# Deep-and-cross ranker on one core: SyncE fetches 13 and ScalarE 8 embedding fields, the biases come by ScalarE, h2's copies are later

## What is computed

```python
x0 = emb[ids].reshape(ids.shape[0], -1)
x = x0
for i in range(cross_w.shape[0]):
    s = x @ cross_w[i]
    x = x0 * s[:, None] + cross_b[i] + x
h = jax.nn.relu(x0 @ w1 + b1)
h = jax.nn.relu(h @ w2 + b2)
h = jax.nn.relu(h @ w3 + b3)
logit = jnp.concatenate([x, h], axis=1) @ out_w + out_b
return jax.nn.sigmoid(logit)
```

## Time and profile before

| | us |
|---|---|
| median of 3 runs | 531.18 (529.99 to 531.2) |
| the profiled execution | 530.56 |
| its span, first to last instruction | 528.8 |
| PE busy | 480.8 (91%) |
| POOL busy | 379.6 (72%) |
| DVE busy | 186.4 (35%) |
| ACT busy | 84.7 (16%) |

### The profile page before, as it was taken

One profiled execution on the slowest core, in us unless ns is written; L12 is line 12 of the kernel. 1 busy time (PEld: TensorE's weight loads), 2 busy tenths in 40 slices (PEclk: granted clock), 3 DMA queues, 4 the chain that ended last, 5 costly groups with the idle time before them and its releaser, 6 DMA issues.

```text
span 528.8 us, 11324 instructions
## 1 busy us (share of the span) xinstructions
PE 480.8 (91%) x2912; PEld 442.2 (84%) x2912; DVE 186.4 (35%) x391; ACT 84.7 (16%) x159; POOL 379.6 (72%) x407
## 2 busy tenths in 40 slices
PE   2699899899999989899898989999899898999997
PEld 1399698898989889798887988888898888989996
DVE  5766414232142423224242321424232142423325
ACT  4642111111011111102011110101111010101111
POOL 5777776777777777777777777777777777777720
PEclk9999999999999999999999999999999999999999
DMA  7971111111111111111111111111111111111100
GB/s 234 387 263 29 28 29 27 28 29 27 29 29 29 28 28 30 29 29 29 27 29 26 30 27 30 26 30 29 26 30 25 30 27 28 27 28 28 28 10 2
DMA packets 19700, 24.90 MB, mean 47 GB/s; under 512 B 9305, under 2 KB 10292, under 8 KB 19636
## 3 DMA queue, kind: packets, MB, share of 16 engines
q0 software_dynamic: 12800, 13.13, 11.2%
q1 hardware_dynamic: 4770, 10.74, 5.7%
q10 hardware_dynamic: 2066, 0.31, 0.3%
HBM read 24.41 MB, written 0.01 MB: 46 GB/s over the span
## 4 chain that ended last, share of the span: by engine, by line
PE 55%; POOL 14%; issue 10%; ACTq 9%; DMA 5%; DVE 4%; ACT 3%; POOLq 0%; DVEq 0%
PE l_bank L717 41%; POOL x_raw L347 14%; ACTq L387 8%; DMA x_raw<-in_L_rec_emb,idx 4%; PE x_bank L717 4%; PE x_bank L729 4%; PE h_bank L771 3%; ACT xT_hi L400 2%; DVE x_raw L516 2%; ACTq L384 1%; PE l_bank L802 1%; DVE xT_lo L523 1%; PE h_bank L741 1%; DVE h2T_lo L528 1%; ACT h2T_hi L411 1%
## 5 line engine op out<-in xcount | busy, mean ns | idle before, releaser
L347 POOL DMA_INDIRECT x_raw<-in_L_rec_emb,idx x400 | 378.8, 947 | 125.5 <-issue 107.7
L717 PE MATMUL l_bank<-w_hi,xT_hi 128*128 128x342 f32 (+1 forms) x624 | 144.9, 333 | 3.5 <-DVE xT_lo L523 3.3
L717 PE MATMUL l_bank<-w_lo,xT_hi 128*128 128x342 f32 (+1 forms) x624 | 137.9, 321 | 0.0
L717 PE MATMUL l_bank<-w_hi,xT_lo 128*128 128x342 f32 (+1 forms) x624 | 137.7, 321 | 0.0
L717 PEld LDWEIGHTS l_bank<-w_hi,xT_hi 128*128 128x128 f32 x624 | 104.0, 191 | 7.9 <-DVE xT_lo L523 5.6
L717 PEld LDWEIGHTS l_bank<-w_lo,xT_hi 128*128 128x128 f32 x624 | 106.8, 191 | 0.0
L717 PEld LDWEIGHTS l_bank<-w_hi,xT_lo 128*128 128x128 f32 x624 | 106.3, 190 | 0.0
L523 DVE TENSOR_TENSOR xT_lo<-x_bank,xT_hi 128x512 fp32r<-128x512 f32 (+1 forms) x66 | 38.2, 578 | 158.5 <-ACT xT_hi L400 158.5
L400 ACT ACTIVATE xT_hi<-x_bank 128x512 fp32r<-128x512 f32 (+1 forms) x66 | 33.5, 507 | 270.3 <-PE x_bank L729 220.4
L729 PE MATMUL x_bank<-identity,x_raw 128*128 128x128 f32 x208 | 34.7, 279 | 27.0 <-DVE x_raw L516 27.0
L729 PEld LDWEIGHTS x_bank<-identity,x_raw 128*128 128x128 f32 x208 | 25.0, 142 | 36.7 <-issue 31.0
(11 more groups left out here) (94 smaller groups left out, 296.5 us busy)
## 6 DMA issues: line engine op xcount, KB each, us to landing
ids<-in_L_rec_emb SPq DMA_DIRECT2D x1152, 0.2 KB
ids<-in_L_rec_emb ACTq DMA_DIRECT2D x896, 0.2 KB
w_raw<-in_L_rec_w SPq DMA_DIRECT2D x18, 512.0 KB, 15.0
x_raw<-in_L_rec_emb,idx POOLq DMA_INDIRECT x400, 2.4
b_rows<-in_L_rec_b SPq DMA_DIRECT2D x1, 512.0 KB
b_rows<-in_L_rec_b SPq DMA_DIRECT2D x1, 256.0 KB
ids<-in_r_ids SPq DMA_DIRECT2D x1, 208.0 KB, 2.7
b_rows<-in_L_rec_b SPq DMA_DIRECT2D x1, 128.0 KB
```

Source lines behind the costliest of these rows:

```text
L347: pool.indirect_dma_start(out=dst, out_offset=None, in_=emb, in_offset=rows).then_inc(landed, 16)
L717: done = pe.matmul(bank[:, 0:b - a], x[:, k, :], w[:, k, a:b], start=(k == 0 and n == 0), stop=(k == last_k and n == 2))
```

## The change

- GpSimd leaves 21 fields to others instead of 16. SyncE takes field 21 of tiles 2 to 14 (13 fields), ScalarE field 20 of tiles 3, 5, 6, 8, 9, 11, 13 and 14 (8). Both lie in chunk 10, the last of group 2. Tile 15 is GpSimd's alone.
- ScalarE's shares become five, `[13, 19, 14, 16, 18]`, 80 rows a step; `fetch` may go over from one field to the next within a share, with a load for each, and stops after 8 x 128 rows.
- The placing copies come behind the copy of group 1 instead of group 2.
- On ScalarE, h2's copy moves from ahead of group 1's copy to behind it and the placing; on VectorE, h2's difference moves from ahead of group 1 to behind it. In the last step both stay.
- The five loads of biases go from SyncE's queue to ScalarE's, ahead of its copy of group 1 in the first step.
- The addresses are made by four instructions instead of three.

```diff
@@ -44,20 +44,21 @@
     LOW_BITS = 2 ** (H.bit_length() - 1) - 1
-    SP_TILES = [2, 4, 6, 8, 9, 10, 12, 14, 15]
+    SP_TILES = list(range(2, TILES - 1))
     SP_REGS = 32
-    SP_FIELD = F - 2
+    SP_FIELD = GROUPS[2][-1] * FPK + 1
     SP_BUFS = 4
-    assert SP_FIELD // FPK in GROUPS[-1] and SP_FIELD // FPK in LAST_GROUPS[3]
-    ACT_TILES = [3, 5, 7, 9, 11, 13, 15]
-    ACT_FIELD = F - 1
+    ACT_TILES = [3, 5, 6, 8, 9, 11, 13, 14]
+    ACT_FIELD = GROUPS[2][-1] * FPK
     ACT_BUFS = 2
-    ACT_SHARES = [8, 12, 4, 16, 12, 12]
-    assert ACT_FIELD // FPK in GROUPS[-1] and all(
-        sum(ACT_SHARES) * (t - 1) >= P * (j + 1) for j, t in enumerate(ACT_TILES)) and P % sum(ACT_SHARES) == 0
+    ACT_SHARES = [13, 19, 14, 16, 18]
+    assert all(sum(ACT_SHARES) * (t - 1) >= P * (j + 1) for j, t in enumerate(ACT_TILES))
+    ONE_RUNS = [(SP_FIELD, range(2, TILES - 1)), (ACT_FIELD, range(3, 10, 3)), (ACT_FIELD, range(5, 15, 3)), (ACT_FIELD, range(13, 14))]
+    AT_ROWS = [(f, t) for f, tiles in ONE_RUNS for t in tiles]
+    assert sorted(AT_ROWS) == sorted([(SP_FIELD, t) for t in SP_TILES] + [(ACT_FIELD, t) for t in ACT_TILES])
     ROW = E * 4
@@ -280,16 +280,14 @@
                 src = {"w1": w1, "w2": w2, "w3": w3}[name][k * P:(k + m) * P, :].rearrange("(m p) c -> p m c", m=m)
                 sync.dma_start(parts(n)[0], src).then_inc(weights_loaded[n], 16)
-            sync.wait_ge(idx_ready, 3)
-            for rows, vec in ((b1_rows, b1), (b2_rows, b2), (b3_rows, b3), (out_w_rows, out_w[D:D + N3, 0]), (out_b_rows, out_b)):
-                sync.dma_start(rows[:, :], vec.rearrange("(o n) -> o n", o=1).broadcast_to([P, rows.shape[1]])).then_inc(rows_loaded, 16)
             sync.wait_ge(sp_idx_ready, 1)
             for i, t in enumerate(SP_TILES):
                 if i >= SP_BUFS:
                     sync.wait_ge(sp_placed, i - SP_BUFS + 1)
                 for p in range(0, P, SP_REGS):
                     regs = [sync.alloc_register(f"sp_row{i}_{p + j}") for j in range(SP_REGS)]
-                    sync.load(regs, at_bytes[at_row[t]:at_row[t] + 1, p:p + SP_REGS])
+                    row = AT_ROWS.index((SP_FIELD, t))
+                    sync.load(regs, at_bytes[row:row + 1, p:p + SP_REGS])
                     for j, reg in enumerate(regs):
                         at = sync.snap(reg, donate=True, min_val=0, max_val=(2 * H - 1) * ROW)
                         sync.dma_start(sp_rows[i % SP_BUFS][p + j:p + j + 1, :].bitcast(U8),
@@ -366,6 +364,11 @@
                 act.wait_ge(weights_loaded[n], 16)
                 act.activation(hi, raw, ACT.Copy).then_inc(hi_split, 1)
+            def load_rows():
+                act.wait_ge(idx_ready, 3)
+                for rows, vec in ((b1_rows, b1), (b2_rows, b2), (b3_rows, b3), (out_w_rows, out_w[D:D + N3, 0]), (out_b_rows, out_b)):
+                    act.dma_start(rows[:, :], vec.rearrange("(o n) -> o n", o=1).broadcast_to([P, rows.shape[1]])).then_inc(rows_loaded, 16)
             def sp_place(t):
                 i = SP_TILES.index(t)
                 act.wait_ge(sp_landed[i % SP_BUFS], 16 * P * (i // SP_BUFS + 1))
@@ -376,17 +379,19 @@
             def fetch(share):
-                j, p = fetched[0] // P, fetched[0] % P
-                if p == 0 and j >= ACT_BUFS:
-                    act.wait_ge(act_placed, j - ACT_BUFS + 1)
-                row = len(SP_TILES) + j
-                regs = [act.alloc_register(f"act_row{j}_{p + i}") for i in range(share)]
-                act.load(regs, at_bytes[row:row + 1, p:p + share])
-                for i, reg in enumerate(regs):
-                    at = act.snap(reg, donate=True, min_val=0, max_val=(2 * H - 1) * ROW)
-                    act.dma_start(act_rows[j % ACT_BUFS][p + i:p + i + 1, :].bitcast(U8),
-                                  emb_bytes[:, bass.DynSlice(at, ROW)], bounds_check="skip_entire_dma").then_inc(act_landed[j % ACT_BUFS], 16)
-                fetched[0] += share
+                while share > 0 and fetched[0] < P * len(ACT_TILES):
+                    j, p = fetched[0] // P, fetched[0] % P
+                    if p == 0 and j >= ACT_BUFS:
+                        act.wait_ge(act_placed, j - ACT_BUFS + 1)
+                    row, rows = AT_ROWS.index((ACT_FIELD, ACT_TILES[j])), min(share, P - p)
+                    regs = [act.alloc_register(f"act_row{j}_{p + i}") for i in range(rows)]
+                    act.load(regs, at_bytes[row:row + 1, p:p + rows])
+                    for i, reg in enumerate(regs):
+                        at = act.snap(reg, donate=True, min_val=0, max_val=(2 * H - 1) * ROW)
+                        act.dma_start(act_rows[j % ACT_BUFS][p + i:p + i + 1, :].bitcast(U8),
+                                      emb_bytes[:, bass.DynSlice(at, ROW)], bounds_check="skip_entire_dma").then_inc(act_landed[j % ACT_BUFS], 16)
+                    fetched[0] += rows
+                    share -= rows
             def act_place(t):
                 j = ACT_TILES.index(t)
@@ -429,6 +434,8 @@
                         split_hi(n)
                         if n == 0:
                             cross_hi()
+                    if g == 1:
+                        load_rows()
                     x_hi(0, g)
                 h1_hi(0)
@@ -436,30 +443,24 @@
                 fetch(ACT_SHARES[0])
                 x_hi(t, 0)
                 fetch(ACT_SHARES[1])
-                h2_hi(t - 1)
-                fetch(ACT_SHARES[2])
                 x_hi(t, 1)
-                fetch(ACT_SHARES[3])
-                x_hi(t, 2)
                 if t in SP_TILES:
                     sp_place(t)
                 if t in ACT_TILES:
                     act_place(t)
+                h2_hi(t - 1)
+                fetch(ACT_SHARES[2])
+                x_hi(t, 2)
+                fetch(ACT_SHARES[3])
+                x_hi(t, 3)
                 fetch(ACT_SHARES[4])
-                x_hi(t, 3)
-                fetch(ACT_SHARES[5])
                 h1_hi(t)
             def last_step(t):
+                assert t not in SP_TILES and t not in ACT_TILES
                 x_hi(t, 0)
                 h2_hi(t - 1)
-                x_hi(t, 1)
-                x_hi(t, 2)
-                if t in SP_TILES:
-                    sp_place(t)
-                if t in ACT_TILES:
-                    act_place(t)
-                for g in range(3, len(LAST_GROUPS)):
+                for g in range(1, len(LAST_GROUPS)):
                     x_hi(t, g)
                 h1_hi_last(t)
                 h2_hi_last(t)
@@ -634,16 +635,13 @@
                 dots_out(0)
                 h1_lo(0)
-            def begin(t):
+            def step(t):
                 make_whole(t, 0)
                 x_lo(t, 0)
                 l2_out(t - 1)
-                h2_lo(t - 1)
                 make_whole(t, 1)
                 x_lo(t, 1)
-            def step(t):
-                begin(t)
+                h2_lo(t - 1)
                 for g in range(2, NG):
                     make_whole(t, g)
                     x_lo(t, g)
@@ -653,7 +651,12 @@
                 l3_out(t - 1)
             def last_step(t):
-                begin(t)
+                make_whole(t, 0)
+                x_lo(t, 0)
+                l2_out(t - 1)
+                h2_lo(t - 1)
+                make_whole(t, 1)
+                x_lo(t, 1)
                 l3_out(t - 1)
                 for g in range(2, len(LAST_GROUPS)):
                     make_whole(t, g)
@@ -690,11 +693,8 @@
             link(dve.tensor_scalar(past[:, 0:QUICK], ids[:, 0:QUICK], float(H), None, ALU.is_ge))
             dve.wait_ge(idx_ready, 3)
             copied = 0
-            for field, tiles in ((SP_FIELD, [t for t in SP_TILES if t % 2 == 0]), (SP_FIELD, [t for t in SP_TILES if t % 2]),
-                                 (ACT_FIELD, ACT_TILES)):
-                every = tiles[1] - tiles[0]
-                assert tiles == list(range(tiles[0], tiles[-1] + 1, every))
-                a, b = (t * F + field for t in (tiles[0], tiles[-1]))
+            for field, tiles in ONE_RUNS:
+                a, b, every = tiles[0] * F + field, tiles[-1] * F + field, tiles.step
                 dve.scalar_tensor_tensor(out=sp_cols[:, copied:copied + len(tiles)], in0=past[:, a:b + 1:every * F], scalar=float(H),
                                          in1=idx[:, a:b + 1:every * F], op0=ALU.mult, op1=ALU.add).then_inc(sp_cols_ready, 1)
                 copied += len(tiles)
@@ -908,7 +908,7 @@
             pe.transpose(h_bank[0][:, 0:VR], vec_rows[:, :], identity[0:VR, 0:VR]).then_inc(vecs_transposed, 1)
             pe.wait_ge(cross_ready, 1)
-            pe.wait_ge(sp_cols_ready, 3)
+            pe.wait_ge(sp_cols_ready, len(ONE_RUNS))
             pe.transpose(x_bank[1][0:ONE_BY_ONE, 0:P], sp_cols, identity[:, :]).then_inc(sp_cols_transposed, 1)
             pe.wait_ge(sp_idx_ready, 1)
             pe.wait_ge(identity_r_set, 1)
```

(1 more changed line is left out.)

## The result

| | before | after |
|---|---|---|
| median | 531.19 us (4 runs) | 557.21 us (4 runs, 556.13 to 560.88) |
| profiled execution, its span | 530.56, 528.8 | 556.13, 554.3 |
| ratio | | 1.0507 [1.0456, 1.0558] |

The change makes the kernel 5.1% slower.

A forecast was written before the change was run, and what follows sets the result against it. GpSimd's gathers bound the kernel, and ScalarE's queue would after the change. First h1 at 54.05, 12 steps of 34.3, step 13 to 498.6, 28.9 and 41.8 give a 569.3 us span; 1.8 more makes 571 us, range 560 to 583.

The forecast's parts named there:

- The bound: Across the steps: GpSimd's gathers bound the kernel before; after the change ScalarE's queue would take its place.
- ScalarE's step, 34.3 us: ScalarE's queue, steps 1 to 12: loads, row DMAs and copies for 80 rows take 34.3 us a step, against 30.5.
- a row under 0.3 us: ScalarE's row fetches: a sign that would show the forecast wrong; it priced a row at 0.325 us.
- Step 13, 32.6 us: Tile 12's h1 to tile 13's: ScalarE-bound for 26.9 us up to group 3's copy, then TensorE for 5.7.
- Step 14 and the end: Tile 13's h1 onward: no ScalarE rows, TensorE's 28.9 us, then an unchanged 41.8 us to the end.
- The later h2: h2's copy and difference behind group 1's: removes TensorE's 1.06 us stall, but gains nothing under the new bound.
- The faster rival: ScalarE's rows fit in a 30.5 us step, GpSimd stays the bound: 524.9 us; chance 0.07.
- Barely slower: Every ScalarE register load hides under the copy ahead, step 31.2 us, time about 535 us; chance 0.05.
- Slower still: Each of ScalarE's five shares loses 0.28 us to irregular row runs: 588 us; chance of over 583, 0.04.
- SyncE and the biases: SyncE's 13 fields cost nothing; bias loads on ScalarE's queue taken as 0, with 3 us kept for the range.
- The rule beside the faster rival: Skill page on DMA issue: issue time is usually small beside the DMA; by it the 524.9 us rival would win.

The follow-up runs named there:

- e3_64_rows: The change with ScalarE's rows cut to 64 a step: six tiles, shares 10, 16, 12, 12, 14; 522.4 us, ratio 0.9838.
- h1_aligned: The change with only ScalarE's shares altered, to 12, 20, 16, 16, 16, still 80 rows a step; 520.7 us, ratio 0.9801.
- g3_chunk_12: e3_64_rows with the fetched fields back in chunk 12 (fields 24 and 25), placed behind group 2's copy; 608.9 us, ratio 1.1488.
- k1_aligned_h2_ahead: h1_aligned with h2's copy and difference back ahead of group 1; 524.6 us, ratio 0.9906.
- h2_chunk_12_aligned: g3_chunk_12 with shares 8, 16, 12, 16, 12 instead of 10, 16, 12, 12, 14; 523.3 us, ratio 0.9859.
- g4_72_rows: The change with 7 ScalarE tiles, shares 12, 16, 16, 13, 15, 72 rows a step; 521.4 us, ratio 0.9826.
- h4_96_rows: h1_aligned with 9 ScalarE tiles, shares 16, 24, 20, 16, 20, 96 rows a step; 518.8 us, ratio 0.9765.
- e2_only_bias: The kernel before with only the five bias loads moved to ScalarE's queue; 531.06 us, ratio 1.0004.
- h3_swapped_fields: The kernel before with the two fields exchanged, ScalarE fetching field 24 and SyncE field 25; 530.3 us, ratio 0.9987.

## Why the prediction was wrong, and where right

**The bound** came out right: in the change ScalarE's 80 rows don't fit as they are loaded, its queue takes GpSimd's place, GpSimd waits for TensorE and a step lasts over 33 us. e3_64_rows and h1_aligned take the bound away from ScalarE in two ways and the time falls below that of the kernel before both times. But the sum had the reason wrong. With its own loads and the rows' true price its step would be 34.3 - 8.3 = 26.0 us, under GpSimd's 30.5; what made ScalarE the bound, the price of unaligned loads, was no term of it. The direction was luck to that extent.

**ScalarE's step, 34.3 us**, is the term that was mis-sized (33.4 in the mean), and its two prices were both wrong. The DMA runs were to take 26.7 us; in the step shown they take 2.26 + 4.53 + 2.98 + 4.76 + 3.85 = 18.4. The 0.325 us a row came from field 25; the change fetches field 20. The inputs were in the reference, and the flag that skips a DMA was in the code; the step that failed was to carry a price over from rows of a different kind. From activation to first DMA the shares were to take 7.4 us; they take 1.34 + 4.22 + 1.60 + 0.77 + 4.29 = 12.2 here. The load's line, 0.25 + 0.06 a register, was drawn through shares that all began at multiples of 4 and was used for some that do not. The errors of 8.3 down and 4.8 up, with 1.3 us of waiting for TensorE ahead of group 0's copy, give 32.1 us in this step. Over steps 1 to 12 the trace has 17.4 us of DMA runs and 14.0 from activation to first DMA in the mean, and 2.0 between a run and the next copy where the sum had 0.25: 33.4. So one error hid the other: with the forecast's row and the true load the step would be longer still (g3_chunk_12 took 37.7 us with 64 rows); with the true row and loads near the forecast's, h1_aligned is faster than the kernel before. The prediction had named the sign itself, "a row under 0.3 us"; it is 17.4 / 80 = 0.22 us.

**Step 13, 32.6 us**, was 29.4: the copy of group 3 came 2.1 us sooner, since two of that step's shares were cheaper than priced with load and rows together, and h1 stood 4.6 us behind it instead of 5.7. Step 14 and the end held within 0.3 us.

**The later h2** was priced at nothing, since TensorE's 28.9 us were not the bound. Under the bound of the change this was not tested. Near GpSimd's bound it is worth 4 us (k1_aligned_h2_ahead), and 27 where long loads stand ahead of h2: the stall of the earlier trace rows grows with the share ahead of it.

**The faster rival** had its condition right (a step under 30.5 us) and its price too small: 524.9 was given, h1_aligned took 520.7. The working took 5 gathers. But tile 15's two came back to GpSimd at the end, where TensorE needs the last of them late, so that up to tile 14 GpSimd has 369 gathers instead of 376: 7 x 1.25 = 8.75 us, 522.4. By the same count the others come to 524.9 (e3_64_rows, 522.4 measured; h2_chunk_12_aligned, 523.3), 523.7 (g4_72_rows, 521.4) and 521.2 (h4_96_rows, 518.8): all lie 1.6 to 2.5 us below it. The kernel before, run beside these, took 530.5 to 530.8 instead of 531.2, which is 0.4 to 0.7 of that; the rest was not taken apart, and the count itself was made after the runs.

**The other rivals.** *Barely slower* had every load hidden under a copy. In the step shown only that of 14 is nearly so (1.60 us behind three copies); those of 19 and 18 stand open for some 4 us. Its sum also kept 32.6 us for step 13, more than its own step of 31.2. *Slower still* feared longer runs of rows; they were shorter.

**SyncE and the biases** at nothing: nothing speaks against it. Among ScalarE's waits in the change there is none for SyncE's rows, and e2_only_bias differs from the kernel before by 0.2 us, within what runs differ. The rule cited there from the Trainium skill, "DMA: Bandwidth & Descriptors", section "Issuing engines are not separate DMA queues", that transfers from all engines interleave, would have allowed up to 3 us; the runs show none.

**The rule beside the faster rival**, in the same section of the Trainium skill (that the issue time is usually small beside the DMA itself), does not describe these transfers. In the kernel before, all packets of ScalarE's queue took 0.3% of 16 engines' span, about 25 us, and its 896 issues at 235 ns took 211 us of ScalarE's queue; how long one row takes to land no profile here shows. In the step shown of the change, 18.4 us went into the runs of 80 issues and 12.2 into the register loads with the copies ahead of them, of 32.1. The same page of the Trainium skill, section "Latency and other measured facts", gives a register load a floor of about 600 ns; here loads of 4 registers took 0.49 us at the least.

## What to carry to other kernels

An engine that is 16% busy on the page can be full: add up what its queue issues between its operations before it is given more. A price per item is good only for items of the same kind; ask what the data make of it (a skipped transfer, an unaligned start) before it is carried to another field, size or offset. Where a share of work is sized against gaps, keep the register loads' starts at multiples of 16 bytes.

## What the runs showed of the hardware

- A register load from SBUF on ScalarE's queue costs 0.25 us and 0.06 a register from a start that is a multiple of 4 elements of 4 bytes (16 registers: 1.2 us), and 0.25 us and about 0.22 a register from other starts (10: 2.45 us, 14: 3.3, 19: 4.4). Making the shares multiples of 4 was worth 36 us between the change and h1_aligned.
- A row DMA whose address is out of bounds, and which is skipped, takes 90 ns to issue on ScalarE's queue and 73 on SyncE's, one that is carried out 235 and 228 ns (medians; h3_swapped_fields against the kernel before).
- TensorE's granted clock fell in the change, 0.975 over the span against 1.0. A row of TensorE's timeline in the kernel after, and two windows (length, busy times, then the granted clock, DMA share, GB/s):

```profile
119.48 0.50 PE L717 MATMUL l_bank<-w_hi,h1T_hi 128*128 128x512 f32 x1 [2.19 <-DVE h1T_lo L529]
...
118.00:126.00 8.00, 6.52 (x24) 5.22 (x25) 3.38 (x7) 1.68 (x3) 4.64 (x5) 0.79 0.10 21
126.00:152.00 26.00, 24.56 (x156) 22.91 (x154) 6.08 (x12) 2.25 (x6) 19.58 (x22) 1.00 0.12 28
```

In the first, TensorE had idled for 2.19 us ahead of layer 2 and the granted clock was 0.79 of 2.4 GHz, so that part of it ran at 1.2 GHz; in the second it was full. A matmul of layer 2 (hi by hi) took 454 ns in the mean over the span; in the kernel before it took 406. What that adds to the time was not taken apart; ScalarE was the bound in those steps.
